# A graph network's gathers from GpSimd: at most two of a block on their way

## The reference

```
edge_index = [src, dst]
msg  = relu(concat(x[src], edge_attr) @ W1.T + b1) @ W2.T + b2      # per edge
agg  = segment_sum(msg, dst)                                        # per node
gi, gh = agg @ Wih.T + bih, x @ Whh.T + bhh                         # a GRU cell
r, z = sigmoid(gi_r + gh_r), sigmoid(gi_z + gh_z)
n    = tanh(gi_n + r * gh_n)
x    = layernorm(x + (1 - z) * n + z * x)

mean = segment_sum(x[dst], src) / max(degree(src), 1)
x    = layernorm(x + mean @ weight + x @ root_weight + bias)
```

## Time and profile before

| what | value |
|---|---|
| time without the profiler, median of three | 4591.73 us |
| span of the profiled execution, first to last instruction | 5892.9 us |
| TensorE busy in it | 4424.1 us (75%) |
| weight loads busy | 3765.1 us (64%) |
| DVE busy | 3327.6 us (56%) |
| GpSimd (POOL) busy | 3209.3 us (54%) |
| ScalarE busy | 2357.5 us (40%) |
| moved by DMA | 998.71 MB |

### The profile page before, as it was taken

The page is one execution under the profiler, slowest core; times in us unless marked ns, Lnnn a source line. Parts: engine busy times, 40 slices in busy tenths (PEclk is TensorE's granted clock), DMA queues, the critical chain, the costliest instruction groups (busy, mean ns, idle before and its releaser), DMA issues.

```text
span 5892.9 us, 89839 instructions
## 1 busy us (share of the span) xinstructions
PE 4424.1 (75%) x30332; PEld 3765.1 (64%) x30332; DVE 3327.6 (56%) x9964; ACT 2357.5 (40%) x4278; POOL 3209.3 (54%) x3198
## 2 busy tenths in 40 slices
PE   6577777777777777777777777777777777777776
PEld 5465666666666666666666666667666666666664
DVE  4444656565656555555656565656565656555555
ACT  2244343434343434344444434343434343434343
POOL 2566555655565555555555656555655555555510
PEclk8667989798978888888888888879797989888889
DMA  6444747575656566565656575647575656566556
GB/s 192 91 127 137 197 141 207 150 200 149 190 162 184 168 174 174 166 184 158 187 156 194 151 201 151 197 141 206 149 202 150 194 158 186 163 179 171 169 146 176
DMA packets 1017762, 998.71 MB, mean 169 GB/s; under 512 B 204167, under 2 KB 857548, under 8 KB 1016921
## 3 DMA queue, kind: packets, MB, share of 16 engines
q1 hardware_dynamic: 830878, 459.88, 28.2%
q10 hardware_dynamic: 84075, 321.56, 17.1%
q0 software_dynamic: 102352, 211.43, 14.6%
HBM read 655.22 MB, written 337.22 MB: 168 GB/s over the span
## 4 chain that ended last, share of the span: by engine, by line
PE 50%; another core or an unknown queue 16%; DVE 15%; issue 10%; ACT 6%; DMA 1%; DVEq 1%; POOL 0%; SPq 0%; ACTq 0%; POOLq 0%
PE stream_pse L1199 12%; PE stream_psa L1208 10%; PE stream_psw L1223 9%; PE stream_pse L1191 6%; PE stream_psw_third L1223 5%; DVE stream_col L969 4%; ACT stream_a_sb L884 4%; DVE stream_sums L979 3%; DVE stream_sums L983 2%; ACT stream_hid L846 1%; DVE ring L947 1%; PE stream_psw L1247 1%; DVE stream_acc L939 1%; DVE stream_row L964 1%
## 5 line engine op out<-in xcount | busy, mean ns | idle before, releaser
L829 POOL DMA_INDIRECT ring<-y,ring x3105 | 3137.7, 1011 | 2314.9 <-ACT stream_hid L846 1492.4
L884 ACT CAST stream_a_sb<-stream_psa 98x512 f16<-98x512 f32 x3125 | 1768.8, 585 | 2909.1 <-PE stream_psa L1208 1125.5
L947 DVE TENSOR_TENSOR ring<-stream_pse,ring 128x384 f32<-128x384 f32 x1250 | 612.2, 490 | 1862.9 <-remote 836.8
L1208 PE MATMUL stream_psa<-stream_col,stream_row 128*98 128x256 f16 x6250 | 1291.4, 311 | 477.6 <-ACT stream_a_sb L884 289.0
L1223 PE MATMUL stream_psw<-stream_z,stream_strip 128*128 128x257 f16 x5850 | 936.4, 293 | 382.4 <-DVE stream_sums L983 333.1
L1208 PEld LDWEIGHTS stream_psa<-stream_col,stream_row 128*98 128x98 f16 x6250 | 823.9, 143 | 623.6 <-issue 392.2
L1199 PE MATMUL stream_pse<-w1b,ring 128*128 128x128 f32 x6250 | 1154.8, 325 | 49.8 <-issue 23.8
L1199 PEld LDWEIGHTS stream_pse<-w1b,ring 128*128 128x128 f32 x6250 | 997.7, 231 | 101.2 <-issue 61.1
L969 DVE TENSOR_TENSOR stream_col<-iota_lo,stream_twin 128x1536 f16<-128x1536 f16 x1250 | 1022.2, 818 | 0.0
L1223 PEld LDWEIGHTS stream_psw<-stream_z,stream_strip 128*128 128x128 f16 x5850 | 594.0, 105 | 542.1 <-issue 306.2
L1191 PEld LDWEIGHTS stream_pse<-stream_seg,stream_hid 128*128 128x128 f32 x6250 | 836.2, 211 | 1.1
(11 more groups left out here) (203 smaller groups left out, 2063.8 us busy)
## 6 DMA issues: line engine op xcount, KB each, us to landing
A<-stream_a_sb ACTq DMA_DIRECT2D x625, 490.0 KB
stream_strip<-A SPq DMA_DIRECT2D x1862, 160.0 KB
ring<-in_ea_blocks_dram SPq DMA_DIRECT2D x625, 160.0 KB
ring<-y,ring POOLq DMA_INDIRECT x3125
stream_col<-A SPq DMA_DIRECT2D x84, 96.0 KB, 2.5
prologue_xt<-in_xT_dram SPq DMA_DIRECT2D x14, 448.0 KB
y<-prologue_ysb SPq DMA_DIRECT2D x14, 448.0 KB
ring<-r SPq DMA_DIRECT2D x49, 128.0 KB, 2.5
```

What stands on the lines that cost most here:

```text
L829: nc.gpsimd.indirect_dma_start(out=yg[s.c % 4][:, t, :], out_offset=None, in_=h.y, in_offset=bass.IndirectOffsetOnAxis(ap=idx[s.c // (PH / ...
L884: nc.scalar.copy(a_sb[s.c % AR][0:RW, j, :], psa[BANK[j]][0:RW, :]).then_inc(a_out, 1)
L947: V.tensor_tensor(yg[s.c % 4][:, lo:hi, :], pse[half][:, 0:(hi - lo) * D].rearrange("p (t d) -> p t d", d=D), yg[s.c % 4][:, lo:hi, :], AL ...
L1208: last = nc.tensor.matmul(psa[BANK[j]][0:RW, e * LOS:(e + 1) * LOS], row1[s.c % 2][:, 2 * j + e, :], col1[s.c % 2][:, 2 * j + e, :], start ...
```

## The change

In a block the gathers t = 0, 2 and 4 now raise `gathered[s.c % 4]` (48 a turn), and t = 1 and 3 raise a new semaphore `gathered_odd[s.c % 4]` (32 a turn). Before it issues t = 2 GpSimd waits until t = 0 of the block has landed, before t = 3 until t = 1 has, and before t = 4 until t = 2 has. t = 0 and t = 1 wait for no gather, so across the border of two blocks up to four can be on their way. The prologue's gathers still raise `gathered` alone, 80 in the first turn, which is why 32 is added to its later values. DVE and the index load of SyncE wait for both semaphores.

```diff
-        gathered = h.gathered
+        gathered, gathered_odd = h.gathered, m.sems("gathered_odd", 4)
...
-                        sp.wait_ge(gathered[b.c % 4], b.turn(4, 16 * BT))
+                        sp.wait_ge(gathered[b.c % 4], b.turn(4, 48) + 32)
+                        reach(sp, gathered_odd[b.c % 4], b.turn(4, 32, 1))
...
                 for t in range(BT):
+                    if t in (2, 4):
+                        pool.wait_ge(gathered[s.c % 4], s.turn(4, 48, 1) + 32 + 8 * t)
+                    if t == 3:
+                        pool.wait_ge(gathered_odd[s.c % 4], s.turn(4, 32, 1) - 16)
                     nc.gpsimd.indirect_dma_start(
                         out=yg[s.c % 4][:, t, :], out_offset=None, in_=h.y,
                         in_offset=bass.IndirectOffsetOnAxis(ap=idx[s.c // (PH // 2) % 2][:, s.c % (PH // 2), t:t + 1], axis=0)
-                    ).then_inc(gathered[s.c % 4], 16)
+                    ).then_inc((gathered_odd if t % 2 else gathered)[s.c % 4], 16)
...
                 if half == 0:
-                    dve.wait_ge(gathered[s.c % 4], s.turn(4, 16 * BT))
+                    dve.wait_ge(gathered[s.c % 4], s.turn(4, 48) + 32)
+                    reach(dve, gathered_odd[s.c % 4], s.turn(4, 32, 1))
```

## The result

The changed kernel takes 6082.5 us (median of four runs, 6070 to 6094) where the kernel before takes 4586.4: a ratio of 1.326 (95% interval 1.324 to 1.328), 1496 us more. On a second chip it was 6073.6 against 4573.5, 1.329 (1.326 to 1.333). The direction was right; the size, forecast at +741 us, is twice that.

A forecast was written before the change was run, and what follows sets the result against it. GpSimd was taken to bound the timed runs. Blocks growing from 6.615 to 7.92 us add 811 us over 621 blocks, less 70 us slack: 4592 + 741 = 5333 us; range 4900 to 5900, for 8 of 10 4680 to 6100.

The forecast's parts named there:

- GpSimd as the bound of the timed runs: Stream gathers: 621 blocks of 6.615 us plus both ends make 4573 us of GpSimd work in the timed 4592.
- The slack of 70 us: GpSimd's spare time in the timed runs, taken between 19 and 122 us and subtracted from the added 811 us.
- The reason given for the 1301 us between span and median: Profiled span 5892.9 us against 4592 us timed: the timed runs were taken to differ by running without the profiler.
- The forecast of a profiled span of 6090 us: Only the 149 blocks without a relu wait pay 1.31 us each, adding 195 us to the profiled span.
- The chain g0, g2, next block: GpSimd's gathers t = 0, t = 2, next block's first: two landing delays plus a 1.32 us step, 7.92 us a block.
- rival (b): The stream's traffic stretches gather landings to 4.2 us: 9.72 us a block, +1858 us, 6450 us; chance 0.16.
- the size of l: Time from a gather's start to the start of one that waited for it: 3.3 us, likely 2.95 to 3.75.
- The 0.22 us for the slower start: Added to the landing because GpSimd starts 0.28 us after a releasing engine's end, TensorE 0.06 us.
- The cost with no rival: Added semaphore waits of DVE (621) and SyncE (39): 0 to 0.05 us each, 33 us at most, off the bound.
- (a): Stream gathers land within 2.65 us, or cost GpSimd less without the profiler, so nothing is late: 4592 us; chance 0.10.
- (c): Fewer gathers in flight shorten landings and the mean gather to 0.944 us: up to 208 us saved, 4384 us; chance 0.04.
- keep their busy times: In the changed kernel's profile, TensorE, DVE and ScalarE were to be busy as long as before.

The follow-up runs named there:

- i1: Changed kernel with its three GpSimd waits deleted, two semaphores kept, traced on chip 5: 4578.6 us against 4572.9 for the kernel before.
- e1: A trace at the slower level; the text given does not say which kernel it is of and gives no time under this name.
- g1: A trace at the slower level, without landing waits, 1468 us of relu wait; the text given does not define it further.
- h1: A trace on a faster chip; the text given does not say which kernel it is of and gives no time under this name.
- experiment 4: Changed kernel with only the waits of t = 2 and 4, without that of t = 3: 6039.2 us (1.022) on chip 2, 6052.1 (1.029) on chip 9.
- Experiments 6 and 7: Stores of A cut after block 36, then all stores of A doubled: changed kernel 5368.8 and 7003.6 us, kernel before 4583.6 and 5107.4 us.
- experiment 1: Changed kernel without its three GpSimd waits, second semaphore kept: ratio 1.001 to the kernel before on chips 2, 9 and 5.
- experiment 9: Kernel before with four gathers a block instead of five, chip 5: 4385.4 us, ratio 0.959.
- experiment 5: Changed kernel with three semaphores in turn, up to three gathers of a block on their way: 5127.7 us against 4566.2 on chip 0, 1.121.
- experiment 3: Changed kernel with only the wait of t = 3 for t = 1: 5530.7 us against 4566.2 on chip 0, 1.210; 0.987 and 0.975 on chips 2 and 9.
- experiment 8: Changed kernel with each of t = 1 to 4 waiting for the gather before it, one on its way: 9296.7 us, 2.032.

## Why the prediction was right in sign and wrong in size

**GpSimd as the bound of the timed runs: right.** The prediction worked it out of durations, as 4573 us of GpSimd work in 4592. Trace i1 shows it: 6.63 us a block, 41 us of relu wait. The slack of 70 us was too much; measured block and floor differ by 0.01 us, under 10 us over the stream.

**The reason given for the 1301 us between span and median: wrong.** "Without the profiler" was an assumption. Runs at either level have a span within 2 us of their time, and the changed kernel's profiled span (6083.3) is its timed one. What differs is the chip, or the session on it: only chip 5 was used in two sessions, with the faster level both times, and for the first trace the chip is not on record. The traces of before, e1 and g1 of the slower level hold 55,000 to 57,000 semaphore updates, those of i1 and h1 on the faster chips 121,000 to 124,000. The number is not one of the chip alone: the kernels with the waits of t = 2 and 4 have 74,000 and 78,000 on chips 2 and 9. Nothing here shows what is cause and what effect. The forecast of a profiled span of 6090 us came near 6083 by chance: it compared a trace of one level with a kernel measured at the other. For the same reason "GpSimd's wait for relu falls towards 700 us" failed (28).

**The chain g0, g2, next block: right.** A block is the sum of two landings and a step. Measured from the starts: g0 to g2 4.03 us, g2 to g4 3.74, g4 to the next g0 1.31, together 9.09. The starts of a block spread over 7.78 us where 6.6 were forecast, just short of the 8 us that the prediction set as the sign of rival (b). The wait of t = 3 costs nearly nothing beside it (the estimate of experiment 4).

**The step that failed is the size of l.** "For TensorE's view of a stream gather I take 3.0 us" was the term; with 0.27 us on top it made 3.3 and twice 3.3. Measured were 4.03 and 3.74, together 7.78 instead of 6.6: 1.18 us more a block, 733 us over 621 blocks. With the slack of 70 us not there, 741 + 733 + 70 = 1544 against the measured 1496; the 48 us between are not accounted for. The 0.22 us for the slower start was right: with TensorE's 0.06 us it makes 0.28 us, and 0.26 were measured from landing to start.

The choice went wrong in two ways. First, the stretch that it leaned on (33 prologue rows, median 2.81) had DMA shares of 0.24 to 0.37; the row at 0.57 with 3.85 us was beside it and was marked down for twice the bytes. Half the bytes save little: the quickest gather of the stream lands in 2.35 us, the quickest of the prologue in 2.64 as TensorE sees it. Second, it took one number where there is a spread. In the changed kernel's trace the gathers that meet no byte of A's store in the 2.5 us after their start land in 2.84 us, those that meet 317 KB or more in 4.33; a chain of waits pays the mean of that. Experiments 6 and 7 confirm the store as cause: mean landings of 2.95, 3.52 and 4.36 us with none, one and two. The price was that of a stream without stores of A: without them g0 to g2 takes 3.25 us and g2 to g4 3.37, and the block of 7.93 us is the 7.92 of the forecast. The 1.16 us a block that the stores add (9.09 - 7.93) are as good as the whole error of the forecast block (9.09 - 7.92 = 1.17). This is the mechanism of rival (b), which was priced at l = 4.2 and given 0.16.

**The cost with no rival: right.** The second semaphore at nothing (experiment 1).

**Rivals.** (a) fails: the quickest gather lands in 2.35 us, a tenth in under 2.44, and the mean is 3.52. With it fails, for this stream, the estimate of 2.15 us for 64 KB by the rule of the Trainium skill (DMA: Bandwidth & Descriptors, "Anatomy of one DMA — SWDGE (gpsimd) path"): no landing counted in the changed kernel's trace is as short. (c) fails: gathers keep 945 ns and 1020 ns on average, as before, with at most two of a block in flight. Its remark that TensorE leaves little room below was right (experiment 9). So was the other side of rival (b), that longer blocks lower the DMA share, but that is worth little: the last gather of a block lands in 3.65 us on average in i1 (253 blocks whose increments are all there, DMA share 0.80 to 0.83) and in 3.43 in the changed kernel (490 blocks, 0.58 to 0.59).

**That TensorE, DVE and ScalarE "keep their busy times": wrong for TensorE.** At the faster level its busy time goes from 3967.8 us (i1) to 4550.7 for the same 30332 matmuls, and its mean granted clock from 0.898 to 0.803. It is not on the path (2% of the chain), so this costs nothing here.

## What to carry to other kernels

A wait for a transfer's landing on an engine that issues transfers in order turns a throughput (one step) into a latency (a landing), and slack in the consumer's buffers does not help, since the issuer itself is the bound; work out the chain of landings per turn and compare it with the present turn. Price a landing from rows beside the same large transfers and from their mean with its tail, not from a quiet stretch; the mean DMA share of a stretch tells little of it (3.65 us at 0.80 to 0.83, 3.43 at 0.58 to 0.59). And when a trace's span and the timed runs differ by more than a percent, do not put it on the profiler: find out first whether both are of the same kind of run.

## What the runs showed of the hardware that was not expected

- The same program without landing waits takes 4.57 ms on chips 0 and 5 and 5.90 ms on chips 2 and 9, steady within 0.5% on each. At the slower level GpSimd idles (1468 us of relu wait in g1, 41 in i1) and the granted clock averages 0.83 to 0.84 against 0.90. What binds there is open.
- The landing of a 64 KB gather of 512-byte rows ranges from 2.4 us to over 5 us with what else is stored meanwhile (a tenth under 2.44, a tenth over 5.17 us), while GpSimd's time for its descriptors stays at a median of 0.94 us in every trace shown here.
- The more TensorE waits, the lower the clock that it is granted and the longer it is busy with the same work. At the faster level its mean granted clock and busy time are 0.898 and 3968 us without waits (i1), 0.874 and 4151 in experiment 5, 0.843 and 4327 in experiment 3, 0.803 and 4551 in the changed kernel, 0.673 and 5431 in experiment 8.
- A longer block lowers the DMA share (0.80 to 0.83 in i1, 0.58 to 0.59 in the changed kernel) and shortens the landing by only some 0.2 us (3.65 to 3.43 us for the last gather of a block), since the gathers still meet the stores of 490 KB:

```profile
500.00:1500.00 1000.00, 914.19 (x7201) 822.68 (x7200) 771.52 (x2342) 542.62 (x964) 769.89 (x756) 0.92 0.83 234
```

```profile
500.00:1500.00 1000.00, 762.54 (x5071) 647.94 (x5072) 548.44 (x1660) 404.40 (x713) 557.72 (x548) 0.80 0.59 167
```

The first row is i1, the second the changed kernel, each from 500 to 1500 us: busy time of TensorE, its weight loads, DVE, ScalarE and GpSimd in the stretch, then TensorE's clock, DMA share and GB/s.
